# A one-core vision tower on Trainium2: coefficient steps spread over later units, and TensorE's squares, means, query and values in another order

## The reference, cut to what matters

```python
reduce_feats = x.mean((3, 5)).reshape(b, c, hw).transpose(0, 2, 1)      # patch means
q = _ln(reduce_feats, ln_q_w, ln_q_b) @ Wq.T
kv = _ln(unf, ln_kv_w, ln_kv_b) @ Wkv.T                                   # every pixel of a patch
attn = softmax(einsum('bhpd,bhpnd->bhpn', q * scale, k), axis=-1)
aggre = einsum('bhpn,bhpnd->bhpd', attn, v)
h = reduce_feats + aggre @ proj_w.T + proj_b
...
def step(carry, f):                       # the state-space layer, s = 1 / (1 + dt*dt*a)
    x_new = s * x - dsa * z + fx
    z_new = ds * x + s * z + fz
h = _layernorm(h + attn_layer(h))
h = _layernorm(h + mixture_of_experts(h))
```

## Time and profile before

| | |
|---|---|
| median of 3 runs | 1020.51 us (1019.67 to 1021.63) |
| the profiled execution's own time | 1021.32 us |
| its span | 1019.5 us |
| PE busy, share of the span | 943.5 us, 93% |
| DVE | 761.7 us, 75% |
| ACT | 501.4 us, 49% |
| POOL | 436.1 us, 43% |
| chain that ended last | PE 82%, DVE 11%, issue 3% |

### The profile page before, as it was taken

One profiled execution on the slowest core, in us unless ns is written; L12 is line 12 of the kernel. 1 busy time (PEld: TensorE's weight loads), 2 busy tenths in 40 slices (PEclk: granted clock), 3 DMA queues, 4 the chain that ended last, 5 costly groups with the idle time before them and its releaser, 6 DMA issues.

```text
span 1019.5 us, 24614 instructions
## 1 busy us (share of the span) xinstructions
PE 943.5 (93%) x9608; PEld 368.8 (36%) x9608; DVE 761.7 (75%) x1290; ACT 501.4 (49%) x799; POOL 436.1 (43%) x259
## 2 busy tenths in 40 slices
PE   4569999999999999999999989996999999999996
PEld 1114344343434334343434443232333333333332
DVE  6678787878778787878878776998566766766664
ACT  3335454554545454454545412265465664655753
POOL 3237676777767677776767720000110100101000
PEclk9769999999999999999999999998899999999999
DMA  9128878787887878787887742000000000000000
GB/s 384 33 65 234 263 212 264 212 247 230 240 257 218 262 214 247 228 241 251 225 256 217 215 110 58 0 1 0 0 12 21 10 10 21 10 16 15 10 22 22
DMA packets 64007, 141.47 MB, mean 139 GB/s; under 512 B 22576, under 2 KB 22576, under 8 KB 55728
## 3 DMA queue, kind: packets, MB, share of 16 engines
q1 hardware_dynamic: 63920, 140.18, 47.1%
HBM read 68.85 MB, written 4.19 MB: 72 GB/s over the span
## 4 chain that ended last, share of the span: by engine, by line
PE 82%; DVE 11%; issue 3%; DMA 1%; POOL 1%; ACT 1%; SPq 0%; DVEq 0%; POOLq 0%
PE ring L798 20%; PE bank_ms L770 11%; PE qp L835 11%; PE bank_sq L770 5%; PE ring L991 5%; DVE sb_prodv L1152 4%; PE ring L1002 4%; PE bank_ms L1032 3%; PE qp L969 2%; PE bank_sq L991 2%; PE ring L985 2%; PE ring L932 2%; PE bank_ms L1002 2%; PE bank_ms L1024 2%; PE bank_sq L1011 1%
## 5 line engine op out<-in xcount | busy, mean ns | idle before, releaser
L798 PE MATMUL ring<-sb_arena,sb_wqkv 64*64 64x512 f32 x2048 | 269.4, 609 | 37.8 <-DVE sb_prodk L1121 20.2
L1152 DVE TENSOR_TENSOR sb_prodv<-ring,sb_wbc 128x1024 f32<-128x1024 f32 x128 | 154.1, 1207 | 32.6 <-PE ring L798 30.2
L1121 DVE TENSOR_TENSOR sb_prodk<-ring,sb_qbuf 128x1024 f32<-128x1024 f32 x128 | 153.4, 1220 | 20.6 <-PE ring L798 18.1
L405 POOL TENSOR_TENSOR sb_rows<-sb_arena 128x2048 f32<-128x2048 f32 x31 | 141.4, 4562 | 14.8 <-DMA sb_arena<-x 14.8
L534 POOL TENSOR_TENSOR sb_parts_q<-sb_arena,sb_const 128x512 fp32r<-128x512 f32 x15 | 15.6, 1040 | 305.6 <-ACT sb_arena L654 305.6
L835 PEld LDWEIGHTS qp<-sb_prodv,sb_tok_w 64*64 64x64 f32 x4096 | 119.6, 133 | 54.7 <-issue 51.4
L835 PE MATMUL qp<-sb_prodv,sb_tok_w 64*64 64x128 f32 x4096 | 128.4, 269 | 2.5 <-DVE sb_prodv L1152 2.5
L577 ACT ACTIVATE sb_xsq<-sb_arena 128x2048 f32<-128x2048 f32 x64 | 118.5, 1899 | 6.9 <-DMA sb_arena<-x 6.9
L798 PEld LDWEIGHTS ring<-sb_arena,sb_wqkv 64*64 64x64 f32 x2048 | 59.1, 133 | 172.9 <-issue 83.4
L501 POOL TENSOR_TENSOR sb_score<-sb_score,sb_smx 128x512 f32<-128x512 f32 x32 | 41.0, 1281 | 105.1 <-DVE sb_smx L1135 105.1
L407 POOL TENSOR_TENSOR sb_rows<-sb_rows 128x1024 f32<-128x1024 f32 x31 | 73.9, 2384 | 2.4
(11 more groups left out here) (198 smaller groups left out, 1489.1 us busy)
## 6 DMA issues: line engine op xcount, KB each, us to landing
sb_arena<-x SPq DMA_DIRECT2D x64, 1024.0 KB, 8.7
sb_wbc<-sb_wgt SPq DMA_DIRECT2D x256, 256.0 KB, 5.7
out<-sb_arena SPq DMA_DIRECT2D x64, 64.0 KB, 1.9
sb_rest_w<-rest_w SPq DMA_DIRECT2D x1, 918.5 KB, 22.1
sb_const<-const SPq DMA_DIRECT2D x1, 520.5 KB, 8.1
sb_tok_w<-tok_w SPq DMA_DIRECT2D x1, 260.5 KB, 2.8
```

The lines of the kernel that those rows point to most:

```text
L405: eng.tensor_tensor(rows[:, :, :, :], pix[:, :, 0:8], pix[:, :, 8:16], ALU.add).then_inc(sum8_ready, 1)
L798: mm = pe.matmul(ring[slot][C * half:C * half + C, i, :], image_block(w, i), x[C * i:C * i + C, m, half, c], start=True, stop=True)
L1121: dve.tensor_tensor(by_pixel(prodk[:, c]), by_pixel(ring[c % 2][:, :, :]), q[:, :, None, :].to_broadcast([P, 2, N_PIX, G32]), ALU.mult).th ...
L1152: dve.tensor_tensor(prodv[:, :, :, G32 * c:G32 * (c + 1)], by_pixel(ring[k % 2][:, :, :]), by_pixel(wbc[:, c]), ALU.mult).then_inc(values_ ...
```

## The change

The change has three parts. (1) The coefficient steps 4 to 15 leave the setup: `free_steps` is called at the end of DVE's step n, behind `pixel_var(n+2)`, by a table: one coefficient step in step 0, two each in steps 1, 2, 3, 28 and 29, one in step 30. (2) `const` is loaded in two parts, the first 529 columns ahead of unit 0's pixels, the other 512 behind `rest_w`; POOL waits for the second part behind the last unit. (3) On PE, `pixel_squares(n+2)` moves ahead of `values` 0, next to `scores(n+1)`; `pixel_means(n+2)` moves ahead of `query(n+2)`; so the values stand in the pairs 0, 1 and 2, 3.

```diff
+FREE_STEPS = {0: (4, 5), 1: (5, 7), 2: (7, 9), 3: (9, 11), 28: (11, 13), 29: (13, 15), 30: (15, 16)}
...
             sp.dma_start(tok_w[:, :], t["tok_w"]).then_inc(tok_in, 16)
+            sp.dma_start(const[:, 0:K_SEL], t["const"][:, 0:K_SEL]).then_inc(const_in, 16)
             load(0)
-            sp.dma_start(const[:, :], t["const"]).then_inc(const_in, 16)
             for u in range(1, NF):
                 load(u)
             sp.dma_start(rest_w[:, :], t["rest_w"]).then_inc(rest_in, 16)
+            sp.dma_start(const[:, K_SEL:K_END], t["const"][:, K_SEL:K_END]).then_inc(select_in, 16)
...
+            pool.wait_ge(select_in, 16)
             pool.tensor_copy(exact[:, H_SEL:H_ONES], const[:, K_SEL:K_END]).then_inc(weights_rounded, 1)
...
-                values(n, m, 0)
                 if nxt2:
                     pixel_squares(n + 2, m2)
+                values(n, m, 0)
                 values(n, m, 1)
                 if nxt2:
+                    pixel_means(n + 2, m2)
                     query(n + 2, m2)
                 values(n, m, 2)
-                if nxt2:
-                    pixel_means(n + 2, m2)
                 values(n, m, 3)
...
             query_scaled(0)
-            free_steps(4, 13)
             pixel_var(0)
...
             query_scaled(1)
-            free_steps(13, L)
-            assert n_coefs[0] == N_COEFS
             pixel_var(1)
...
                 if nxt2:
                     pixel_var(n + 2)
+                if isinstance(n, int):
+                    free_steps(*FREE_STEPS.get(n, (0, 0)))
```

More of the change, by code:

```diff
@@ L198, in build @@
         tok_in = sem("tok_in")
+        select_in = sem("select_in")
         rest_in = sem("rest_in")
@@ L1267, in _ @@
             pipeline(dve, step, UNITS)
+            assert n_coefs[0] == N_COEFS
             tokens(UNITS - 1, (UNITS - 1) % NF)
```

## The result

The changed kernel takes 1102.47 us (median of 4 runs, 1100.58 to 1103.42), the kernel before 1020.62 us beside it: slower by 8.0%, ratio 1.080 with a 95% interval of 1.078 to 1.082. I had forecast 1093 us, range 1070 to 1114, with a chance of 0.96 for slower. The profiled execution has a span of 1098.7 us, 79.2 more than the 1019.5 of before.

The account below looks back on a forecast made before the run. The prediction took a ring of waits between PE and VectorE to bound each unit. Setup -23.0, order +42.1, moved steps +36.8 and +2, clock +14.3 gave +72.2 on 1021.3: 1093 us, range 1070 to 1114.

Parts of the forecast that it names:

- The setup: Ahead of unit 2: with the coefficient steps off the path, K1 of unit 2 comes at 54.1 instead of 77.14, -23.0 us.
- the load of `const`: At the start: first half ahead of unit 0's pixels delays the first patch sums 0.6 us, unit 1 gains it; 0 net.
- The order: On PE in each unit: a block of means ahead makes the query 1.71 us later; +1.45 us a unit, +42.1.
- the form changes alone: On PE: by the tiling-mode rule alone, two changes fewer would save some 0.2 us a unit, 6 us in all.
- The held coefficient steps: On VectorE behind `pixel_var`: GpSimd's `patch_sums` holds moved instructions; step 0 costs 5.6 us, steps 1, 2, 3, 28 7.8 each.
- the dearer case: In step 0: if L1084, the `tensor_tensor`, lost its gap to GpSimd's L409, that step would cost 1.4 us more.
- this instruction always slips in: On VectorE: L1084, the `tensor_tensor`, was taken to fit between two GpSimd instructions; no row showed it held.
- The clock behind the stalls: On PE behind five stalls: lower clock for 5.7 us of dense work, half lost, 2.85 each; +14.3 us.
- Rival 1: Lower clock in ordinary units too, from two waits, 2.1 us together: +17, 1110 us; chance 0.18.
- 1048 (not held): Moved steps on VectorE get the port between GpSimd instructions; steps and clock shrink to 8.6: 1048 us; chance 0.07.
- 1043 (query hidden): The later query on PE is hidden, as when `query_var`'s input isn't what VectorE waits for: 1043 us; chance 0.05.
- the faster one: VectorE, 25% idle, catches up ahead of K0, K1 and K2; only setup and form-change savings stay: 990 us; chance 0.03.

Follow-up runs that it names:

- The two order experiments: Kernel before with only the means moved ahead of the query: 1091.37 us; kernel before with only the squares moved next to the scores: 1022.97 us.

## Why the prediction was right, point by point

- **The setup, -23.0 forecast, -21.5 measured.** Right in its mechanism: PE's waits there are 1.35 to 1.72 us and the clock stays up. That it stayed up was in part luck: with the like of these waits it fell in the kernel with only the coefficient steps, and cost 2.5 us. The 1.5 us that lack are for the most part the load of `const`, which I had put at 0 with a bound of 0.6. Unit 0's squares start at 11.04 us instead of 8.93, and the query's matmuls at 16.91 instead of 15.28. The step that failed is "264 KB at 418 GB/s is 0.6 us": in the five traces with this edit the squares start at 10.15 to 12.02 us, in seven of the eight without it at 8.72 to 8.93, in the eighth at 9.60. What is behind the difference stays open. So does a second spread: in the four kernels with the short setup and without this edit the query's matmuls start at 15.2 in all, yet `pixel_var(0)` at 21.19 to 22.73, since the block of means takes 2.61 to 3.64 us.
- **The order, +1.45 a unit forecast, +1.475 measured.** The later query and the wait that takes its place on VectorE are as forecast (idle 1.42 to 1.58 ahead of `query_var`; K0 1.66, K1 0.37). The query is 1.67 us later (7.30 less 5.63; I had 1.71), and from it to K1 it takes 5.71 us instead of 5.91 (202.34 to 208.05). The two order experiments show that the means ahead of the query are the cause, and the one with the query first that the second pair adds a cost of its own once the query is early, 0.3 us a unit. My sentence that their saving is spent while PE waits was half of it. What I had reckoned from the form changes alone, 6 us less, is out: with the squares' move, which saves the same two a unit, the ordinary period gains 0.03 us.
- **The held coefficient steps, 5.6 and 7.8 forecast.** Step 0's three instructions fill 56.06 to 61.59, 5.5 us, and step 1's six 7.67. Two experiments settle that GpSimd's instructions beside them are the cause: away from these they take 0.2 us, at the change's own place too. In step 0 the `tensor_tensor` did not lose its gap (61.39 for 0.16), so the dearer case that I had worked out by the Trainium skill (SBUF — State Buffer, Who interferes with whom) did not arise there. But my reading that this instruction always slips in was wrong. In step 3 the `scalar_tensor_tensor` fell into a gap and the `tensor_tensor` was held instead, as that section's rule has it:

```profile
148.11 0.22 DVE L1086 SCALAR_TENSOR_TENSOR sb_cv<-sb_cv,sb_sv,sb_cacc 128x2 f32<-128x2 f32 x1
148.21 0.72 POOL L414 TENSOR_TENSOR sb_sum<-sb_rows 128x256 f32<-128x256 f32 x1 [0.16 <-POOL sb_rows L411]
148.37 0.58 DVE L1087 TENSOR_TENSOR sb_cz<-sb_cz,sb_cv 128x2 f32<-128x2 f32 x1
```

- **The clock behind the stalls, +14.3 forecast, about +10 measured** (46.9 less 36.5 held: 5.5, then 7.7 to 8.0). All five stalls brought the lower clock, also the 5.3 us one. The term was mis-sized: I took 5.7 us of matmuls at half speed. The clock is low for longer than that, 6.9 us at four stalls and 10.3 at one, but a part of it passes while PE still waits. Within it PE is busy for 5.2, 3.0, 5.3, 2.7 and 4.7 us, and half of these 20.9 is 10.5, the measured term. I had also misread: before 713.5 the clock was low already, from 705.6 on. In the kernel with only the coefficient steps the same term is 1.8 to 2.0 us a stall (25.15 and 27.3 to 27.45 less 17.78 and the held 5.5 or 7.7).
- **Rival 1, chance 0.18, came true in part, +8.1 us.** Nine of 24 ordinary periods are longer than 19.3 us, five of them by about 1.6 us; at 208.2 the clock is at its lower level for 3.4 us. That the forecast was off by only 9 us is in part luck: the errors are +1.5 (setup), +0.7 (order), -4.2 (steps and the clock behind them), +9.6 (ordinary units) and -0.6 (end), which makes +7.0 in the span; the other 2 us are that the profiled execution, 1100.58 us, is 1.9 below the median. What I gave against it, that an idle of 2.45 us had left the clock alone, was one case and did not carry. In the kernel with the query ahead of the means, where the two waits are 0.49 and 0.37 us, no ordinary unit before 600 us shows it.
- The other rivals are out: 1048 (not held) and 1043 (query hidden) by the lines above, and the faster one, since VectorE's slack at K0, K1 and K2 is still nil.

## What to carry to other kernels

A small instruction that is moved off the setup's path is not free in the loop: look at what GpSimd does beside it at the new place, and put it where its own engine waits and GpSimd is idle. In a loop that two engines pace by turns, as here, a block moved ahead of the one input that the other engine waits for in program order costs most of its length in each round (1.48 of 1.71 us), however idle both look by their shares. Before grouping work on one engine, follow which result the next engine takes first, and make that first.

## What the runs showed of the hardware that I had not expected

- PE's clock fell in ordinary units whose waits are only 1.66 and 0.37 us with 1.09 us of matmuls between, and stayed low for 3.2 to 3.4 us each time, at a cost of about 1.6 us; it had stayed up through a single wait of 2.45 us. In the setup it fell in one trace and stayed up in others with the same waits, 1.3 to 1.7 us. What decides it no run shows.
- At a stall of 5.3 to 7.7 us the lower clock began before the wait was over: 4 us before in step 1 (88.6 and 92.38). Only the part of it that meets matmuls costs time, 2.7 to 5.3 us of 6.9 to 10.3.
- A small VectorE instruction from SBUF to SBUF that starts while a GpSimd `tensor_tensor` runs was held to its end, a `tensor_tensor` too: 0.58 us in step 3 and 1.25 us at 50.29 in the kernel with the steps ahead of `query_var`, instead of 0.16.
- A load of 264.5 KB put ahead of unit 0's pixels delayed their landing: 10.15 to 12.02 us in five traces with it, 8.72 to 8.93 in seven of eight without it and 9.60 in the eighth. From the seven that is 1.2 to 3.3 us, twice to five times its 0.6 us at the 418 GB/s of the earlier trace rows. No experiment here says why.
- A delay of 2.1 us at the start cost nothing that ten runs could tell in the kernel before; in its trace TensorE got its higher clock back 3.2 us sooner by the span's time. In the kernel without the long setup the same edit left 3.2 us in the trace.
